# New durations, occupancies and a shorter hop in the table that orders a layer-norm, attention and feed-forward kernel

## What is computed

```python
x = x + LN(attn(LN(x)))
x = x + LN(ffn(LN(x)))

def attn(x):                      # norms are taken over the last axis
    q = silu(x @ Wq1 @ Wq2)
    a = exp(log_sigmoid(sigmoid(x @ Wk1 @ Wk2)))
    v = x @ Wv
    h = scan: h[n] = a[n] * h[n-1] + (1 - a[n]) * v[n]     # along the 512 positions
    out = q * h
    out = out * rsqrt(mean(out**2) + eps) * norm_w
    return out @ Wo

def ffn(x):
    for i in range(6):
        x = gelu(x @ W1[i].T + B1[i]) @ W2[i].T + B2[i] + x
        if i < 5:
            x = LN(x) * LN_G[i] + LN_B[i]
    return x
```

## Time and profile before

| | us |
|---|---|
| median of three runs (656.38 to 657.34) | 656.39 |
| profiled execution, its own time | 656.95 |
| its span, first to last instruction | 655.2 |
| PE busy | 637.2 |
| DVE busy | 448.2 |
| ACT busy | 409.7 |
| POOL busy | 284.2 |
| mean granted clock of TensorE | 0.998 |

### The profile page before, as it was taken

The page is one execution under the profiler, slowest core; times in us unless marked ns, Lnnn a source line. Parts: engine busy times, 40 slices in busy tenths (PEclk is TensorE's granted clock), DMA queues, the critical chain, the costliest instruction groups (busy, mean ns, idle before and its releaser), DMA issues.

```text
span 655.2 us, 8823 instructions
## 1 busy us (share of the span) xinstructions
PE 637.2 (97%) x3015; PEld 530.1 (81%) x3015; DVE 448.2 (68%) x747; ACT 409.7 (63%) x678; POOL 284.2 (43%) x253
## 2 busy tenths in 40 slices
PE   7898999999999999999999999999999999999996
PEld 5677788888888888888888888888888888888886
DVE  6778665678567767758765777677687757764635
ACT  4988986788756555557555575555675545564433
POOL 6988442669516611338232175212372321222203
PEclk9999999999999999999999999999999999999999
DMA  8120000001101200003000021000020000000001
GB/s 283 66 97 1 1 1 1 1 1 66 65 0 48 82 1 2 0 1 117 13 2 0 1 64 66 1 1 1 0 66 1 0 2 0 2 1 32 33 1 66
DMA packets 8685, 19.36 MB, mean 30 GB/s; under 512 B 1600, under 2 KB 4672, under 8 KB 8640
## 3 DMA queue, kind: packets, MB, share of 16 engines
q1 hardware_dynamic: 8352, 18.53, 8.4%
q10 hardware_dynamic: 288, 0.26, 0.1%
HBM read 16.69 MB, written 2.10 MB: 29 GB/s over the span
## 4 chain that ended last, share of the span: by engine, by line
PE 89%; POOL 5%; issue 3%; DVE 1%; ACT 1%; DMA 0%; POOLq 0%; ACTq 0%; DVEq 0%
PE BK L457 43%; PE BK L742 39%; PE BK L566 2%; PE BK L752 2%; POOL WL L344 1%; POOL QB L551 1%; POOL SB L575 1%; PE BK L431 1%; PE BK L612 1%; PE BK L579 0%; POOL WL L298 0%; DMA X<-in_x 0%; PE BK L792 0%; PE BK L629 0%; ACT R L384 0%
## 5 line engine op out<-in xcount | busy, mean ns | idle before, releaser
L728 ACT ACTIVATE HH<-BK,B 128x512 fp32r<-128x512 f32 x192 | 132.4, 690 | 203.7 <-PE BK L457 203.3
L734 DVE TENSOR_TENSOR HL<-BK,HH 128x512 fp32r<-128x512 f32 x192 | 131.0, 684 | 82.6 <-ACT BK L731 82.2
L457 PE MATMUL BK<-XH,WL 128*128 128x512 f32 x416 | 163.7, 393 | 0.0
L457 PE MATMUL BK<-XH,WH 128*128 128x512 f32 x416 | 162.3, 390 | 0.0
L457 PE MATMUL BK<-XL,WH 128*128 128x512 f32 x416 | 162.0, 389 | 0.0
L742 PE MATMUL BK<-HH,WL 128*128 128x512 f32 x368 | 146.7, 399 | 0.0
L742 PE MATMUL BK<-HL,WH 128*128 128x512 f32 x368 | 143.7, 390 | 0.0
L742 PE MATMUL BK<-HH,WH 128*128 128x512 f32 x368 | 143.2, 389 | 0.0
L731 ACT ACTIVATE BK<-BK,B 128x512 f32<-128x512 f32 x192 | 125.6, 654 | 0.0
L457 PEld LDWEIGHTS BK<-XH,WH 128*128 128x128 f32 x416 | 78.1, 188 | 17.0
L457 PEld LDWEIGHTS BK<-XL,WH 128*128 128x128 f32 x416 | 78.2, 188 | 16.1
(11 more groups left out here) (121 smaller groups left out, 823.3 us busy)
## 6 DMA issues: line engine op xcount, KB each, us to landing
STG<-in_w SPq DMA_DIRECT2D x24, 512.0 KB, 3.7
out<-R SPq DMA_DIRECT2D x16, 128.0 KB, 1.9
X<-in_x SPq DMA_DIRECT2D x3, 512.0 KB, 7.8
R<-in_wv SPq DMA_DIRECT2D x1, 512.0 KB, 5.8
STG<-in_wo SPq DMA_DIRECT2D x1, 512.0 KB, 6.2
X<-in_x ACTq DMA_DIRECT2D x2, 128.0 KB, 3.0
X<-in_x SPq DMA_DIRECT2D x2, 128.0 KB, 2.8
R<-in_wq SPq DMA_DIRECT2D x1, 256.0 KB, 3.3
```

What stands on the lines that cost most here:

```text
L457: r = e.matmul(dst, s, m, start=first and i == 0, stop=last and i == len(todo) - 1)
L728: lambda e, ev=ev, hs=hs, bias=bias: e.activation(HH[:, hs, :], bank_of[ev][:, :], ACT.Gelu, bias=bias),
L734: lambda e, ev=ev, hs=hs: e.tensor_tensor(HL[:, hs, :], bank_of[ev][:, :], HH[:, hs, :].bitcast(f32), ALU.subtract), ("hlo", n, j))
```

## The change

Three things change in the planner, and one key:

- `LASTS` gets new numbers, for more names. For instance a PE product goes from 1.36 to 1.52 by the engine's entry, `zk` and `zq` from 0.69 to 0.84, `turn` from 0.88 to 0.6, `rms` from 0.45 to 0.6, `_nm` from 0.42 to 0.6.
- A new table `FREE` says how much earlier than its result an engine can begin its next operation. Until now this was zero on each engine.
- `HOP` goes from 0.21 to 0.07, and a DMA issue takes 0.45 instead of 0.1.
- The key of `warm` goes from -98 to -96.5.

```diff
-LASTS = {"sync": 0.1, "scalar": 0.6, "vector": 0.68, "gpsimd": 1.31, "tensor": 1.36,
...
-HOP = 0.21
+LASTS = {"sync": 0.45, "scalar": 0.62, "vector": 0.68, "gpsimd": 1.3, "tensor": 1.52,
...
+FREE = {"sync": 0.0, "scalar": 0.11, "vector": 0.09, "gpsimd": 0.05, "tensor": 0.16}
+HOP = 0.07
...
-        clock[e] = t + (0.1 if done in moved else lasts(e, done))
+        spent = 0.45 if done in moved else lasts(e, done)
+        clock[e] = t + spent - FREE[e]
         if done:
             issued.add(done)
-            ends[done] = clock[e]
+            ends[done] = t + spent
             if done in moved:
-                wire = max(wire, clock[e]) + moved[done] / RATE
+                wire = max(wire, t + spent) + moved[done] / RATE
...
-        op("scalar", -98, [("one",)], lambda e: e.activation(WARM[:, :], ONE[:, :], ACT.Gelu), ("warm",))
+        op("scalar", -96.5, [("one",)], lambda e: e.activation(WARM[:, :], ONE[:, :], ACT.Gelu), ("warm",))
```

15 lines of the change are left out of this document (10 added, 5 removed).

## The result

The changed kernel takes 662.97 us (median of four runs, 661.02 to 664.49) against 656.47 us (656.38 to 657.34) for the kernel before on the same chip: a ratio of 1.0094, 95% interval [1.0066, 1.0122]. It is slower by 6.5 us. The forecast was 652.6 us and its range ended at 656.8, so the sign was wrong and the time lies outside the range. The profiled execution of the kernel after took 663.09 us with a span of 661.3 us.

The account below looks back on a forecast made before the run. The prediction took PE as the bound, with room only in its waits before 72 us. It carried 3.3 us left at the `l3` transposes plus 0.5 from the loop: 656.39 - 3.8 = 652.6 us, range 650.8 to 656.8.

Parts of the forecast that it names:

- What bounds the kernel: PE is full from 72 to 590 us; the gain must come from seven waits before 72 us, 11.0 us in all.
- Part 1: First products: PE's wait for `UL` ends earlier, first `zq` at about 13.35 us in place of 14.65, gain 1.3 us.
- Part 2: POOL's weights and first `o`: first `proj` at about 26.95 us in place of 28.41, gain 1.46 us, a delay just covered.
- Part 3: `proj` block 3 and ACT's bound: second tile's first `proj` at 54.4 us in place of 55.83, net gain 2.3 us.
- The first rival: ACT waits 2 us, not 0.5, between 35 and 54 us, so `proj` starts as before; 655.2 us, chance 0.20.
- Part 4: First `l3` transposes: start at 63.75 us in place of 67.46, net gain 3.3 us, the term carried into the sum.
- Part 5: Loop from 72 to 590 us: `mu` and `va` one group earlier without waits, gain 0 to 0.6 us, taken as 0.5.
- The slower rival: Loop: `va` too early in 19 tiles, collisions beside weight pieces in four; 657.0 us or 661.4 with both, chance 0.14.
- The rule against it: DVE and POOL share ports as an exclusive lock, so a denser plan makes more collisions; weighed as the slower rival.
- The chances: Faster 0.48 + 0.10 + 0.12 = 0.70, the last from half the case at ACT; slower 0.10, same 0.20.

Follow-up runs that it names:

- e8: Kernel before with one POOL move: the second tile's second `o` directly ahead of `l2_nb`; 660.49 us against 657.27, ratio 1.0049.
- e11: Changed order up to the second tile's first transposes, old order up to `mm1` of step 4, then changed with `va` of four tiles one group later; ratio 1.0052.
- e14: Kernel before with the first `u` on PE, `ulo` and `q` on DVE, and the first tile's first two `o` on POOL moved earlier; ratio 1.0004.
- e18: The e17 kernel with one more POOL move: the first tile's `l3_nb` ahead of the second tile's block 1 sum; ratio 0.9996.
- e13: Kernel after with 26 idle matmuls on PE in the last transposes ahead of the second tile's first `proj`; 661.82 us, ratio 1.0077.
- e3: Kernel after with `va` of tiles 3, 7, 11 and 15 one group later on PE; ratio 1.0074.
- e10: Order and banks of the kernel before up to `mm1` of step 4, order of the kernel after from there; 659.81 us against 656.82, ratio 1.0047.
- e5: Kernel after with the second tile's second `o` and both `wp_lo` 4 weight pieces behind `l2_nb` on POOL; median 664.43 us, ratio 1.0103.
- e6: The e5 kernel with ACT's `t2` and `a` of block 3 behind the four `l2_nm`, and the later `va` of e3; ratio 1.0074.
- e7: Kernel after with `HOP` back at 0.21, the other changes kept; ratio 1.0046.
- e17: Kernel before with the moves of e14, plus `o` of block 3 and the sums of blocks 2 and 3 ahead of POOL's weight pieces; ratio 0.9992.
- e1: Kernel after with one POOL move: the second tile's `o` of block 1 behind the first tile's `l2_nb`; ratio 1.0088.

## Why the prediction was wrong

**What bounds the kernel** was read rightly: nothing is to be had behind 72 us, and PE's waits ahead of it are the only room. What was missing is that PE's waits there are not separate. The kernels of the table that have the old order from the second tile's transposes up to the loop show it: whatever the lead at 14, 27, 44 or 51 us, the lateness of the second tile's first `proj` is that of `mm1` of step 1 within 0.5 us (e8 to e11, e14 to e18).

**Part 1** held at its point: the first `zq` at 13.37 us (forecast 13.35). **Part 2**: the cover that I called "just" enough was not: the second tile's transposes waited 0.67 us for `l1_nm` (25.41), the first `proj` came at 27.65 and not 26.95, the second tile's `zq` at 35.37 and not 34.25.

**Part 3** is the step that failed, "with 0.5 us of waits for PE and POOL on the way I take 54.3". In the kernel after ACT ran from the second tile's first `tq` at 37.23, not 35.55, because `zq` was 1.1 us late and ACT still had `ohi` and `osq` ahead of the `tq` (1.7 us in all); its 34 instructions took 18.68 us, not 18.26 (0.4); and it idled for 2.3 us, not 0.5 (1.8). That makes 58.2 in place of 54.3. The first rival, "given back at ACT", had 2 us of waits as its condition, which is what came; but it was priced from the early start. I counted what the order put ahead of `l2_nm` on ACT, but took POOL to be idle ahead of `l2_nb`, so that an `o` put there was free. In the new order two weight pieces stand there as well, 3.9 us with the `o` at their normal length, and the collisions add 2.7. In the old order this one `o` ahead of `l2_nb` costs 3.2 us (e8). The first half of the part was misread as well: "`o` of block 3 no longer queues behind three `wp_lo`". It stood behind two weight pieces and a sum before and still does (the pieces take 3.02 us, from 36.08 on), `olo` ended at about 44.3 in place of 41.7, and `proj` of block 3 came at 44.40 and not 42.8.

**Part 4** built on 54.4 and fell with it (68.53 in place of 63.75). 4.0 of these 4.8 us are the late `proj`; the rest is about what `x1` lost beside a scan (4.25 us, and 3.25 in e13). PE's wait for `l3_nm` did go, but `l3_nb` came at 66.07 us, later than before and not at 61.5.

**Part 5** had the right mechanism and the wrong cover. In quiet tiles "a slack of 0.85 us for each, and no wait" held: neither `mu` nor `va` waits there, and the waits of `mu` beside weight pieces went as I said. Beside weight pieces I gave `va` the slack of a quiet tile, although showed what DVE loses there. Up to three waits of 0.9 to 1.04 us follow: 2.2 us net in the profile, about 1.2 us by the mean of eight executions and by e3's median, and 3.0 us by e10's median for the whole loop. The slower rival had named this collision at up to 1.1 us for each of four tiles, but made it depend on 19 small waits that never came, and gave the whole case 0.14.

**The rule against it** stood in the text with no price and too wide. Ahead of `l2_nb` the new order did make more collisions: POOL's 53 instructions from 8 to 72 us take 57.02 us in place of 54.90. Over the whole kernel it made fewer: DVE is busy for 442.0 us in place of 448.2 and POOL for 280.7 in place of 284.2, with the same instructions. What counts is whether a collision falls on the chain that PE waits for. **The clock** was in no term, and no run shows that it should have been: it cost the kernel after nothing visible at 58 us. **The chances**: "of the case at ACT half" is 0.10 and not the 0.12 in the sum for faster, so that 0.68 was meant; it changes nothing.

Together: e8 (3.2 us, a move of POOL ahead of `l2_nb`) and e10 (3.0 us, the loop; 2.0 in its trace) add up to the 6.2 of the ratio. That may be chance: e10's interval runs from 2.1 to 4.1 us, and nothing proves that the stage ahead of the loop is that one move. In e5 and e6, where it is undone within the new order, the time stays, since other queues take its place. So the loss ahead of the loop, 3.6 us at `mm1` of step 4, is located but, within the new order, not undone by any run. Open are also its last 1 us, between 113 and 195 us, where one wait of PE stands (0.42 us at 162.44), and the one wait of e7 at 183.51 us.

## What to carry to other kernels

When one engine starves behind queues of three others, a wait taken from its timeline is not a term of a sum: ask which queue is next, and print each queue up to the instruction that ends the wait, on every engine of the chain. A planner that knows one duration for each operation can pack two engines tightly just where they hinder each other. Leave the order slack beside weight traffic, as the late `va` does; a table with a longer time for these operations was not tried here. And moving a single small step (a norm's 0.2 us bias) behind one 1.3 us product cost 3.2 us, so what feeds many waits goes first in its queue, whatever the plan's clock says.

## What the runs showed of the hardware

- DVE and POOL hold each other up in whole instructions, even for tiny ones: a POOL step of 128x4 elements took 1.12 us beside a scan and 0.20 without; the scan itself took up to 2.33 in place of 1.22.
- TensorE's granted clock fell to 1.2 GHz in or right behind stands of PE of 2.5 to 5.5 us, and also behind shorter ones: in the kernel after at 28.3 us, behind stands of 0.67 and 1.17 us. It stayed at 2.4 GHz through stands of 3.21 us (e17) and 3.38 us (e5), and when 6 us of idle matmuls filled the stand (e13). One and the same order and stand (2.46 us) was seen with the fall (e10) and without (the kernel before).
- Products of `proj` start 0.21 us apart at the low clock and 0.12 at the high. What a fall costs depends on who is late next: nothing where PE has to wait for another engine all the same (the kernel after at 58 us, e10), and about 1.5 us in e1, an estimate: its l3 transposes began at 70.41 us and could have begun 0.14 us behind `l3_nm`, at 68.93.
